# Two last-group steps of a graph layer with a mixture of experts moved forward, and its last block loaded, added and written in halves

## The chip, the cores and the metric

The kernel runs on one core of a Trainium2 chip. Its time is the device time of one launch in microseconds (us). Three timed runs of the kernel before gave 549.81, 551.37 and 551.41 us, median 551.37. A difference of under about 0.3% (1.65 us) can't be told from no change here.

## The reference

`x` has 4096 rows (nodes) of 256 values; `adj` is a 4096 by 4096 matrix of 0 and 1. Everything is float32.

```
x = x + gnn(layernorm(x), adj)
    # mask = adj > 0;  agg = mask @ h / max(row sums, 1)
    # relu(concat(h @ W_self + b_self, agg @ W_nb + b_nb) @ W_comb + b_comb)
x = x + ffn(layernorm(x))
    # logits = h @ Wg + bg;  top 2 of 8 experts, w = softmax of the two logits
    # y_e = gelu(h @ W1[e] + b1[e]) @ W2[e] + b2[e];  sum over the two of w * y_e
```

## The kernel before, in words

**Tiles and groups.** The 4096 rows are 32 tiles of 128 rows. Four tiles are a group (B = 4), and there are NG = 8 groups, numbered 0 to 7. "The last group" is group 7 (tiles 28 to 31), "the group in front" is group 6 (tiles 24 to 27).

**First stage: the graph layer and the routing.** Each engine has its own program, in which a function `main_step` is called once per step, and each call does one piece of work for several tiles at different ages (tile t-3, tile t-5 and so on). For each group, once its logits are there, four things happen in this order:

- *choose* (VectorE, `choose`, L911 to L926) finds the two best experts of each row. Its fourth instruction writes `dgap`, the gap of the two logits; its last ones write `both` and `base`, from which ranks are made.
- *powers* (GpSimd, `powers_of_e`, L555) computes e to the power of `dgap` into `egap`.
- *ranks* (TensorE, L1186 to L1189) are three small matmuls that count, for each row, how many rows before it go to the same expert.
- *slots* (VectorE, `slots`, L935 to L948) needs powers and ranks. It writes the two weights of each row and `slot`, the two places in the memory `dispatched` to which the row goes. It releases the semaphore `slots`.

Then GpSimd issues *dispatches* (L545): per tile two indirect DMAs of 128 rows of 260 values each, so eight per group. On GpSimd all of this stands in one list, made by a loop over s; before, the powers of group k come at step s = 4(k+3), that is s = 40 for group 7, behind the eight dispatches of group 6.

**Second stage: the experts.** The dispatched rows are worked off in ET = 39 expert tiles of 256 rows. Expert step t does, on TensorE: the transposes of tile t (L1211), the first product of tile t-1 (L1224), the second product of tile t-2 (L1239). VectorE copies transposed tiles (`exT`, L1028), makes low parts (L1042) and adds the bias (L1036); ScalarE does the gelu (L699), the high part (L704) and the weighting (L688). GpSimd scatters the weighted outputs to `pair_out` (L595, two indirect DMAs per tile). SyncE loads expert tiles (L466). The first EA = 9 tiles hold only rows of the first half of the groups, so they can run before the last groups are dispatched; from tile 9 on SyncE waits for all dispatches, for eight writes of pad rows (`write_pad`, L352 and L353, 260 KB each), and for the second part of a table that VectorE makes in its expert steps 1 to 4 (`table_late`, L990 to L1013). The pad writes in turn wait for `padrow`, the first instruction of `table_late(0)` (L990).

Where the two stages meet, two constants set the order: EARLY_PE = 2 expert steps stand on TensorE ahead of the last ranks, and EARLY_DVE = 1 on VectorE ahead of the last slots. TensorE's expert step 2 waits for the semaphore `slots` of the last group:

```
if known == EARLY_PE:
    pe.wait_ge(s_slot, NG)
```

**End.** For each group, SyncE waits for the scatters, loads the pairs of the group (`load_pairs`, L478, 1024 KB, from `pair_out` into one of four buffers), VectorE adds them to `x_sb` in two instructions (`combine`, L1066 and L1068), and SyncE writes the group out with four DMAs of 128 KB (`write_out`, L483). After the last group nothing else is left to do.

## Time and profile before

| | us |
|---|---|
| profiled execution, its time | 551.93 |
| profiled execution, its span | 550.1 |
| median of three timed runs | 551.37 |
| TensorE busy | 439.9 (80%) |
| VectorE busy | 391.1 (71%) |
| GpSimd busy | 288.2 (52%) |
| ScalarE busy | 272.6 (50%) |

The span is the time from the first to the last record of one profiled execution; 1.8 us of the execution's time lie around it. The page shows TensorE full from 50 us to 350 us (graph layer) and again from 400 us to 500 us (experts), with a thin stretch between, in which the routing of the last groups ends, and a thin end. The views of the next sections but one are timelines of one engine each: start, length, engine, line, operation, tiles, and in brackets how long the engine was idle before the row and what released it.

### The profile page before, as it was taken

The numbers are of one execution on the slowest core, as the hardware profiler recorded it, in microseconds if no ns is written. First come the engines' busy times: TensorE is split into PE (matmuls) and PEld (weight loads), VectorE is DVE, ScalarE is ACT, GpSimd is POOL, SyncE is SP. The second block draws the span as 40 slices with busy tenths as digits, with TensorE's granted clock in tenths as the row PEclk, the third lists the DMA queues.
The fourth block names the chain that finished last, engine by engine and source line by source line (L and its number), as shares of the span: only waits on it lengthen the run. The fifth ranks groups of instructions, "written<-read, shape, count | busy, mean of one in ns | idle before, by whom it ended". The sixth has DMA issues, their size and how long they took to land.

```text
span 550.1 us, 13137 instructions
## 1 busy us (share of the span) xinstructions
PE 439.9 (80%) x4321; PEld 382.9 (70%) x4321; DVE 391.1 (71%) x1197; ACT 272.6 (50%) x435; POOL 288.2 (52%) x305
## 2 busy tenths in 40 slices
PE   0015999999999999999999999635599999997730
PEld 0014889899898989898988898524378888786520
DVE  5717855686588888878857887574677777679871
ACT  3675452364255353654434444322367777776530
POOL 3993223234156575756564752646545556564570
PEclk9999999999999999999999999955989999999975
DMA  9975999999989999999996944512555555588565
GB/s 248 251 238 119 270 291 298 272 256 269 240 252 250 284 271 308 268 296 271 270 285 184 282 141 139 183 39 98 185 182 163 161 157 156 156 291 342 184 203 153
DMA packets 46785, 122.49 MB, mean 223 GB/s; under 512 B 8953, under 2 KB 18045, under 8 KB 45568
## 3 DMA queue, kind: packets, MB, share of 16 engines
q1 hardware_dynamic: 28896, 68.02, 47.4%
q0 software_dynamic: 16080, 50.49, 28.5%
q10 hardware_dynamic: 1744, 3.15, 2.1%
q8 instruction: 37, 0.61, 0.5%
q14 instruction: 28, 0.23, 0.1%
HBM read 96.52 MB, written 26.93 MB: 224 GB/s over the span
## 4 chain that ended last, share of the span: by engine, by line
PE 33%; DVE 15%; issue 15%; DMA 14%; POOL 13%; ACT 6%; SPq 1%; DVEq 1%; ACTq 1%; another core or an unknown queue 1%; POOLq 0%
PE bank L1224 8%; PE bank L1239 7%; PE bank L1115 5%; PE bank L1116 5%; DMA stage<-in_adj_dram,gidx 5%; POOL dispatched L545 4%; POOL stage L534 4%; DMA wst<-in_L_ffn_W_dram 4%; PE bank L1124 3%; PE bank L1211 2%; DMA stage<-in_adj_dram 2%; POOL z_lo L560 2%; DVE mask L769 2%; DMA x_sb<-in_x_dram 1%; DVE maskT L776 1%
## 5 line engine op out<-in xcount | busy, mean ns | idle before, releaser
L1115 PE MATMUL bank<-z_flat,maskT 128*128 128x257 f16 x1024 | 226.7, 273 | 0.0
L1116 PE MATMUL bank<-z_lo,maskT 128*128 128x256 f16 x1024 | 226.7, 273 | 0.0
L595 POOL DMA_INDIRECT pair_out<-rows,enum x78 | 80.9, 1038 | 64.8 <-DVE gate L1055 34.2
L534 POOL DMA_INDIRECT stage<-in_adj_dram,gidx x64 | 66.2, 1034 | 86.4 <-PE bank L1124 41.6
L1115 PEld LDWEIGHTS bank<-z_flat,maskT 128*128 128x128 fp8e4 x1024 | 100.2, 98 | 12.2
L1116 PEld LDWEIGHTS bank<-z_lo,maskT 128*128 128x128 fp8e4 x1024 | 100.2, 98 | 11.5
L545 POOL DMA_INDIRECT dispatched<-rows,slot x64 | 70.3, 1098 | 26.5 <-issue 19.2
L648 ACT ACTIVATE rows<-bank,rdeg 128x256 f16<-128x256 f32 x32 | 15.1, 473 | 134.3 <-DVE rdeg L829 110.7
L622 ACT ACTIVATE mask<-stage,m 128x2048 fp8e4<-128x2048 int32 x32 | 64.4, 2013 | 20.0 <-DMA stage<-in_adj_dram,gidx 17.9
L1224 PE MATMUL bank<-stage,w 128*128 128x256 f16 x468 | 61.3, 284 | 12.8 <-DVE stage L1028 11.0
L1239 PE MATMUL bank<-w,stage 128*128 x468 | 60.5, 278 | 9.9 <-DVE stage L1042 5.7
L577 POOL TENSOR_TENSOR rs<-ve,mhalf 128x1 f32<-128x1 f32 x32 | 34.9, 1091 | 61.2 <-DVE ve L853 60.1
L1239 PEld LDWEIGHTS bank<-w,stage 128*128 128x128 f16 x468 | 43.8, 99 | 24.6 <-issue 18.4
L699 ACT ACTIVATE stage<-bank,b1c,sc 128x256 f32<-128x256 f32 x78 | 40.2, 559 | 41.3 <-PE bank L1224 28.2
L1224 PEld LDWEIGHTS bank<-stage,w 128*128 x468 | 45.3, 101 | 20.6 <-issue 14.4
L1124 PE MATMUL bank<-wf,aT 128*128 128x256 f16 x384 | 47.2, 273 | 6.4 <-ACT aT L654 6.4
L776 DVE STREAM_TRANSPOSE maskT<-mask 128x1024 uint32<-128x1024 uint32 x32 | 39.9, 1245 | 13.7 <-ACT mask L622 10.5
L1124 PEld LDWEIGHTS bank<-wf,aT 128*128 128x128 f16 x384 | 37.2, 98 | 11.7 <-ACT aT L654 7.4
L769 DVE TENSOR_SCALAR mask<-stage 128x2048 fp8e4<-128x2048 int32 x32 | 39.2, 1226 | 7.4 <-DMA stage<-in_adj_dram 7.3
L688 ACT ACTIVATE rows<-rows,gate 128x256 f32<-128x256 f32 x78 | 35.1, 497 | 16.9 <-DVE rows L1036 13.2
L1028 DVE COPY stage<-bank 128x1024 f16<-128x1024 f16 x39 | 26.9, 690 | 23.1 <-PE bank L1224 16.7
L1042 DVE SCALAR_TENSOR_TENSOR stage<-stage,shs 128x512 f16<-128x512 f32 x39 | 29.2, 749 | 11.2 <-ACT stage L704 9.4
(175 smaller groups left out, 636.5 us busy)
## 6 DMA issues: line engine op xcount, KB each, us to landing
stage<-in_adj_dram SPq DMA_DIRECT2D x128, 256.0 KB
stage<-dispatched SPq DMA_DIRECT2D x39, 260.0 KB
wst<-in_L_ffn_W_dram SPq DMA_DIRECT2D x16, 256.0 KB
z_lo<-pair_out SPq DMA_DIRECT2D x4, 1024.0 KB
maskT<-pair_out SPq DMA_DIRECT2D x4, 1024.0 KB
out_dram<-x_sb SPq DMA_DIRECT2D x32, 128.0 KB
dispatched<-pad SPq DMA_DIRECT2D x15, 260.0 KB
x_sb<-in_x_dram SPq DMA_DIRECT2D x6, 256.0 KB, 9.1
```

What stands on the lines that cost most here:

```text
L534: gp.indirect_dma_start(out=stage[:, s, b - 2, :], out_offset=None, in_=adj_q[:, :], in_offset=bass.IndirectOffsetOnAxis(ap=gidx[:, 0:1], ...
L545: gp.indirect_dma_start(out=xs_dram[:, :], out_offset=bass.IndirectOffsetOnAxis(ap=slot[:, t, c:c + 1], axis=0), in_=rows_f[:, t, :], in_o ...
L595: gp.indirect_dma_start(out=yp_dram[:, :], out_offset=bass.IndirectOffsetOnAxis(ap=enum[:, a, s:s + 1], axis=0), in_=ysb[:, a, s, :], in_o ...
L622: sc.activation(mask[:, u % 2, 2:4, :], stage[:, s], ACT.Sigmoid, bias=m100[:, 0:1], scale=200.0, saturate=False).then_inc(s_mA, 1)
L699: sc.activation(ehid[:, u % 2, h, :], hps[2 * (u % 2) + h][:, 0:TT], ACT.Gelu, bias=b1c[:, bass.ds(ex, 1), h], scale=sc1[:, bass.ds(ex, 1) ...
L769: v.tensor_scalar(mask[:, u % 2, 0:2, :], stage[:, s], 0.0, None, ALU.is_gt, saturate=False).then_inc(s_mD, 1)
L776: v.transpose(maskT32[u % 4], mask32[u % 2]).then_inc(s_T, 1)
L1115: mm(acc[u % 2][:, 0:D + 1], a, z_hi[:, i, :], start=(i == 0), stop=False)
L1116: last = mm(acc[u % 2][:, 0:D], a, z_lo[:, i, :], start=False, stop=(i == NT - 1))
L1124: last = mm(out_, lhs(xp * KT + kt), w(wp, kt), start=(first and n == 0), stop=(final and n == 3 * KT - 1))
L1224: last = mm(hps[2 * r + h][:, 0:TT], w, exT[:, r, (xp * KT + kt) * TT:(xp * KT + kt + 1) * TT], start=(n == 0), stop=(n == 3 * KT - 1))
L1239: last = mm(fold[r][:, s * H:s * H + H], ehl[:, r, xp, kt, s * P:s * P + P], w, start=(n == 0), stop=(n == 3 * KT - 1))
```

## The change

The change has three parts.

1. On GpSimd the powers of group 7 stand at step s = 37, behind the powers of group 6 and ahead of the eight dispatches of group 6.
2. On TensorE the ranks of group 7 stand behind expert step 0 and ahead of expert step 1; before, they stood behind expert step 1. The wait for `slots` stays at expert step 2.
3. The pairs of group 7 are loaded in two DMAs of 512 KB with a semaphore each, added in two times two instructions of half the size, and written in two times four DMAs of 64 KB, the first half from SyncE, the second half from ScalarE.

```diff
-        LAST_RANKS, EARLY_PE, EARLY_DVE = NT + PR - B, 2, 1
+        LAST_RANKS, EARLY_PE, EARLY_DVE = NT + PR - B, 1, 1
...
+        def write_half(eng, h):
+            eng.wait_ge(s_o2, NG + h)
+            t = NT - B + h * B // 2
+            for g in range(G):
+                eng.dma_start(out_v[g, NG - 1, :, h * B // 2 * D:(h + 1) * B // 2 * D],
+                              x_sb[Q * g:Q * g + Q, t:t + B // 2, :].rearrange("p e d -> p (e d)")).then_inc(s_out, 16)
...
-                sp.dma_start(yin[k % Y].rearrange("p e k n -> p (e k n)"), yp_v[k]).then_inc(s_yl[k % Y], 16)
+                if k < NG - 1:
+                    sp.dma_start(yin[k % Y].rearrange("p e k n -> p (e k n)"), yp_v[k]).then_inc(s_yl[k % Y], 16)
+                else:
+                    for h in range(2):
+                        sp.dma_start(yin[k % Y][:, h * B // 2:(h + 1) * B // 2].rearrange("p e k n -> p (e k n)"),
+                                     yp_v[k, :, h * B * D:(h + 1) * B * D]).then_inc((s_yl[k % Y], s_yh)[h], 16)
...
-            for k in (NG - 2, NG - 1):
-                write_out(k)
-            sp.wait_ge(s_out, 16 * G * NG)
+            write_out(NG - 2)
+            write_half(sp, 0)
+            sp.wait_ge(s_out, 16 * G * (NG + 1))
...
+            LAST_POWERS = NT + X1
             sent = 0
             for s in range(GATE_STEPS + 1):
...
-                if s >= 12 and s % B == 0:
+                if s >= 12 and s % B == 0 and s // B - 3 < NG - 1:
                     powers_of_e(s // B - 3)
+                if s == LAST_POWERS:
+                    powers_of_e(NG - 1)
...
             for t in range(ET - GATED, ET):
                 gate_rows(t)
+            write_half(act, 1)
...
-            for k in range(len(COMBINE), NG):
+            for k in range(len(COMBINE), NG - 1):
                 combine(k)
+            for h in range(2):
+                dve.wait_ge(*((s_yl[Y - 1], 16 * (NG // Y)), (s_yh, 16))[h])
+                t, es = NT - B + h * B // 2, slice(h * B // 2, (h + 1) * B // 2)
+                xh_ = x_sb[:, t:t + B // 2, :]
+                v.tensor_tensor(xh_, xh_, yin[Y - 1][:, es, 0, :], ALU.add).then_inc(s_o1, 1)
+                dve.wait_ge(s_o1, NG + h)
+                v.tensor_tensor(xh_, xh_, yin[Y - 1][:, es, 1, :], ALU.add).then_inc(s_o2, 1)
...
-                if known == EARLY_PE:
+                if known == 2:
                     pe.wait_ge(s_slot, NG)
```

GpSimd, at the dispatches of groups 6 and 7. Before (the four dispatches ahead of the powers of group 7, the powers, the first dispatches of group 7):

```order
L545 DMA dispatched<-rows,slot 36608x260 [waits slots,hi2,lo2]
L545 DMA dispatched<-rows,slot 36608x260
L545 DMA dispatched<-rows,slot 36608x260 [waits slots,hi2,lo2]
L545 DMA dispatched<-rows,slot 36608x260
L555 TENSOR_TENSOR egap<-ebase,dgap 128x4 [waits logit_gaps]
L545 DMA dispatched<-rows,slot 36608x260 [waits slots,hi2,lo2]
L545 DMA dispatched<-rows,slot 36608x260
```

The same place now; the row with x2 holds the powers of groups 6 and 7, and the dispatches behind it are those of group 6, with those of group 7 right behind them (`rs` is the inverse deviation of the second layernorm):

```order
L592 TENSOR_TENSOR rs<-ve,mhalf 128x1 [waits variance2] x2
L568 TENSOR_TENSOR egap<-ebase,dgap 128x4 [waits logit_gaps] x2
L558 DMA dispatched<-rows,slot 36608x260 [waits slots,hi2,lo2]
L558 DMA dispatched<-rows,slot 36608x260
L558 DMA dispatched<-rows,slot 36608x260 [waits slots,hi2,lo2]
L558 DMA dispatched<-rows,slot 36608x260
```

The powers of group 7 moved ahead of eight dispatches, and the sixteen dispatches of the two groups now follow one another.

TensorE, where the two stages meet. Before: transposes of expert tile 0, transposes of tile 1, the first product of tile 0 (L1224, of whose rows the first two and the last one are shown), the last ranks (L1186 to L1189), then expert step 2 with its wait for `slots`:

```order
L1211 MATMUL bank<-ident,stage 128x128 [waits expert_rows_loaded0,expert_lo,tables]
L1211 MATMUL bank<-ident,stage 128x128 x7
L1211 MATMUL bank<-ident,stage 128x128 [waits expert_rows_loaded1]
L1211 MATMUL bank<-ident,stage 128x128 x7
L1224 ISA [waits e_transposed_copied]
L1224 MATMUL bank<-stage,w 128x256
L1224 MATMUL bank<-stage,w 128x256
L1186 MATMUL bank<-both,upper 128x32 [waits expert_scales,one_hots]
L1187 MATMUL bank<-base,ones 128x32
L1189 MATMUL bank<-base,ones 128x8
L385 TENSOR_LOAD tab [waits slots]
```

The same place now, with the product cut in the same way:

```order
L1236 MATMUL bank<-ident,stage 128x128 [waits expert_rows_loaded0,expert_lo,tables]
L1236 MATMUL bank<-ident,stage 128x128 x7
L1211 MATMUL bank<-both,upper 128x32 [waits expert_scales,one_hots]
L1212 MATMUL bank<-base,ones 128x32
L1214 MATMUL bank<-base,ones 128x8
L1236 MATMUL bank<-ident,stage 128x128 [waits expert_rows_loaded1]
L1236 MATMUL bank<-ident,stage 128x128 x7
L1249 ISA [waits e_transposed_copied]
L1249 MATMUL bank<-stage,w 128x256
L1249 MATMUL bank<-stage,w 128x256
L385 TENSOR_LOAD tab [waits slots]
```

The ranks moved ahead of the transposes of tile 1 and of the first product; the wait for `slots` stayed behind that product.

## Rows read from the trace of the kernel before

**Rows 1.** Windows: busy us (x) of PE PEld DVE ACT POOL, PEclk, DMA share, GB/s.
```profile
360.00:380.00 20.00, 6.40 (x60) 5.13 (x60) 9.67 (x55) 5.31 (x9) 10.38 (x11) 0.50 0.15 55
...
410.00:420.00 10.00, 9.59 (x99) 8.12 (x97) 7.30 (x18) 7.77 (x16) 5.60 (x7) 1.00 0.61 167
```

**Rows 2.** Timeline of GpSimd, 366 to 391 us, in part.
```profile
366.72 1.03 POOL L545 DMA_INDIRECT dispatched<-rows,slot  x1 [2.82 <-DVE slot L948]
...
376.69 1.04 POOL L555 TENSOR_TENSOR egap<-ebase,dgap 128x4 f32<-128x4 f32 x1
380.14 1.02 POOL L545 DMA_INDIRECT dispatched<-rows,slot  x1 [2.41 <-DVE slot L948]
...
388.04 1.35 POOL L545 DMA_INDIRECT dispatched<-rows,slot  x1 [0.30 <-issue]
389.69 0.97 POOL L545 DMA_INDIRECT dispatched<-rows,slot  x1 [0.30 <-issue]
```

**Rows 3.** Timeline of VectorE, 367 to 392 us, in part.
```profile
367.03 0.17 DVE L913 TENSOR_TENSOR dgap<-top 128x4 f32<-128x4 f32 x1
...
369.70 0.68 DVE L1028 COPY stage<-bank 128x1024 f16<-128x1024 f16 x1
377.77 0.17 DVE L935 TENSOR_SCALAR wden<-egap 128x4 f32<-128x4 f32 x1 [7.39 <-POOL egap L555]
...
379.15 0.17 DVE L948 CAST slot<-slotf 128x8 int32<-128x8 f32 x1
380.69 0.74 DVE L1042 SCALAR_TENSOR_TENSOR stage<-stage,shs 128x512 f16<-128x512 f32 x1
...
381.68 0.16 DVE L990 TENSOR_TENSOR padrow<-cntt,region 128x8 int32<-128x8 f32 x1
...
387.14 1.41 DVE L1003 TENSOR_TENSOR z_lo<-tio,z_lo 128x1200 f32<-128x1200 f32 x1
...
391.95 0.69 DVE L1028 COPY stage<-bank 128x1024 f16<-128x1024 f16 x1 [1.98 <-remote]
```

**Rows 4.** Timeline of TensorE, 366 to 392 us, in part.
```profile
366.09 1.89 PE L1211 MATMUL bank<-ident,stage 128*128 128x128 f16 x16
370.52 2.74 PE L1224 MATMUL bank<-stage,w 128*128 128x256 f16 x12 [2.54 <-DVE stage L1028]
373.05 0.23 PE L1186 MATMUL bank<-both,upper 128*128 128x32 f16 x1
...
380.03 1.03 PE L1211 MATMUL bank<-ident,stage 128*128 128x128 f16 x8 [6.71 <-DVE slot L948]
...
387.71 0.71 PE L1239 MATMUL bank<-w,stage 128*128 x5
...
391.79 0.60 PE L1239 MATMUL bank<-w,stage 128*128 x4 [0.45 <-issue]
```

**Rows 5.** Timeline of ScalarE, 374 to 392 us, in part.
```profile
374.12 0.72 ACT L704 ACTIVATE stage<-stage,shs 128x512 f16<-128x512 f32 x1
...
392.21 1.02 ACT L699 ACTIVATE stage<-bank,b1c,sc 128x256 f32<-128x256 f32 x2 [7.18 <-remote]
```

**Rows 6.** SyncE's instructions of line 352, 384 to 392 us.
```profile
L352 SPq SEQ_ASSERT  x3: 14/649/699, 383.6 to 391.0; - x3
```

**Rows 7.** Waits of SyncE's queue, whole span, one row.
```profile
SPq L463 <- DVE tab L1013: 3.8, 1, 3.8
```

**Rows 8.** Timeline of all engines, 535 to 546 us.
```profile
535.45 0.99 POOL L595 DMA_INDIRECT pair_out<-rows,enum  x1 [0.30 <-issue]
537.75 0.34 SPq L478 DMA_DIRECT2D maskT<-pair_out  x1
538.14 9.81 SPq L483 DMA_DIRECT2D out_dram<-x_sb  x8
543.73 1.22 DVE L1066 TENSOR_TENSOR x_sb<-x_sb,maskT 128x1024 f32<-128x1024 f32 x1 [8.31 <-DMA maskT<-pair_out]
544.98 1.23 DVE L1068 TENSOR_TENSOR x_sb<-x_sb,maskT 128x1024 f32<-128x1024 f32 x1
```

More of the change, by code:

```diff
@@ L291, in gnn_moe_kernel @@
         s_ysc = [sem(f"outputs_scattered{i}") for i in range(RY)]
-        s_padr = sem("pad_places")
+        s_padr, s_yh = sem("pad_places"), sem("last_half_of_pairs_loaded")
         s_g2, s_gt = sem("gate_steps"), sem("outputs_weighted")
```

## The prediction

> **What bounds the kernel now.** I read the page's slices and the windows first, then the chain of waits, then each engine's timeline where the chain leaves TensorE. Through most of the span TensorE is the bound, in the expert stage too: in 410 to 420 us it is busy 9.59 of 10 us at a granted clock of 1.00 [rows 1]. Two stretches are not its own. From 360 to 380 us it is busy 6.40 of 20 us at a clock of 0.50 [rows 1], and there the chain runs over GpSimd: the slots of group 7 start only at 377.77, after VectorE has idled 7.39 us for `egap` [rows 3], which GpSimd makes at 376.69, behind the eight dispatches of group 6 that began at 366.72 [rows 2]. TensorE idles 6.71 us for these slots before the transposes of tile 2 at 380.03 [rows 4]. The second stretch is the end: last scatter 535.45 to 536.44, pairs of group 7 asked for at 537.75, added from 543.73 to 546.21 [rows 8], span over at 550.1, 3.9 us later.
>
> A third feature decides how much of the first stretch comes back. From about 387 to 392 us engines stand still though what they wait for is there. TensorE has done five of twelve matmuls of a second product at 388.42 and does the last four at 391.79 [rows 4]; ScalarE is idle 7.18 us until 392.21, though its input, the first half of the product that ended ahead of TensorE's row of 387.71, was ready at about 387.1 [rows 4, 5]; a check on SyncE's sequencer that can take 14 ns takes 649 and 699 ns [rows 6]; a copy on VectorE waits 1.98 us until 391.95 [rows 3]. The first pad writes and the last dispatches (389.69 plus 0.97 us, [rows 2]) are under way together there. It ends about a microsecond after the last dispatch.
>
> **Part 1, powers ahead of the dispatches.** `dgap` of group 7 is ready at 367.03 + 0.17 = 367.20 [rows 3]. The powers now start there and take 1.04 [rows 2], to 368.3. The dispatches of group 6 start 0.3 later, at 368.6 instead of 366.72: 1.9 us late. Nobody waits for them but the tiles from 9 on, which wait for all dispatches. Eight of them at 0.97 + 0.30 us give 378.8 for the first dispatch of group 7, instead of 380.14: 1.3 us early, since the 2.41 us of waiting and the 1.04 us of powers go and 1.9 us come. The last dispatch ended at 390.66; it now ends at 389.3, or at about 390.1 if two more of them are as slow as the one of 1.35 us.
>
> That slow dispatch at 388.04 ran beside a VectorE instruction with two inputs, 387.14 to 388.55 [rows 2, 3]. The Trainium skill ("SBUF — State Buffer", "SBUF: two separate sides") says that such a VectorE instruction and a GpSimd operation that reads the same memory lock each other out entirely. By that rule this dispatch would end 0.97 after 388.55, at 389.52; it ended at 389.39, so the trace nearly agrees. By that rule moving sixteen dispatches beside VectorE's table work gives back up to 0.8 of the 1.3 us; without it the 1.3 us stay. It doesn't change the slots.
>
> **Part 2, ranks ahead of the first product.** Before, the ranks stood at 373.05, behind the product of 370.52 [rows 4]; with the powers at 368.3 they would have been the next wait. Now they start when VectorE's choose is done, about 369.8, and take some 0.3. TensorE's transposes of tile 1 (half of 16 in 1.89 us, or 1.03 for eight at 380.03, [rows 4]) now stand behind them, so the first product starts at 371.1 instead of 370.52: 0.6 late. VectorE's copy of tile 0 (369.70 to 370.38) keeps its place, then the slots take 379.32 - 377.77 = 1.55 [rows 3]: ready at 372.0 instead of 379.32, 7.3 early.
>
> What is late next is the chain of tile 0: its high part ended at 374.12 + 0.72 = 374.84 on ScalarE [rows 5], now at 375.4, and the low part on VectorE, which stood at 380.69 [rows 3], follows at 375.5. That is 5.2 early. TensorE's transposes of tile 2 follow the product at 373.9, 6.1 early, and wait no more. `padrow` (381.68, [rows 3]) and with it the pad writes are 5.2 early too. So 5.2 us reach the standstill.
>
> **The standstill.** Its place in the work is fixed by the pad writes, 5.2 early; its end, if it hangs on pads and dispatches together, by the last dispatch, which is only 1.3 early. I can't price this from one row, so both ends: 5.2 us if it travels with the work and keeps its length, 1.3 if nothing moves until the dispatches are out. I take 3.0, nearest to ScalarE's row, since the chain goes through ScalarE there: its instruction went 5.1 us after its input was ready, not never. Input ready 5.2 early (381.9) plus 5.1 gives 387.0; its gelus and high part take 1.9 free, and three more such 0.65 us delays bring them to 390.9, where before they ended at 394.07. That is 3.2; TensorE's row alone (three matmuls in 3.4 us) would give some 1.7. Hence 3.0.
>
> Behind it nothing else is known to hold the work: tile 9's load waited last for the table, 3.8 us [rows 7], and the table is VectorE work of expert steps 1 to 4, so it moves with the rest; in the full stretch [rows 1] a shift stays a shift.
>
> **Part 3, halves.** Before, the adding took 2.48 us behind the whole load [rows 8]. An instruction of 512 elements costs between half of 1.22, 0.61, and 0.74, the low part's [rows 8, 3]. Two for the first half run while the second half still comes in; two for the second, some 1.4 us, stay behind the end of the load: 1.1 us saved. The last four writes carry half the bytes and start from ScalarE, idle by then; their issue (546.21 to 547.95, [rows 8]) keeps its 1.7 us, the last landing saves perhaps 0.2. Sum 1.3. Lower bound: both halves land together and all four additions stay, about -0.1. Upper: 2.0, if the shorter second load also lands sooner. The extra DMA issue costs 0.34 us ahead of group 6's writes [rows 8], which aren't last.
>
> Issue to first addition was 5.98 us for 1024 KB, beside 512 KB of writes [rows 8]. The Trainium skill ("DMA: Bandwidth & Descriptors", "Anatomy of one DMA — SWDGE (gpsimd) path") gives a DMA a fixed 2.0 us and the rest by bytes at 436 GB/s. By it 512 KB would be in after 3.2 us and 1024 KB after 4.4, so halves would lead by 1.2 us, a little short of the 1.4 that the first two additions need; the saving would be 0.9. The trace's longer time speaks for more lead. It is stated for GpSimd's DMAs, and no row here shows a half by itself.
>
> **Sum.** 3.0 + 1.3 = 4.3 us off the profiled execution's 551.93: 547.6. That execution stands 0.56 above the median of the runs, so for the median 551.37 - 4.3 = 547.1.
>
> **Rivals.**
> 1. *The standstill travels with the work.* It needs a cause in the work or the pads alone. For it: it begins behind the first pad writes, and dispatches alone don't stop TensorE's product at 370.52 [rows 4]. Against: it ends with the dispatches. 5.2 + 1.3 = 6.5, to 544.9.
> 2. *The standstill is a wall.* Everyone resumes behind the last dispatch: 1.3 + 1.3 = 2.6, to 548.8; 549.6 with the slow dispatches.
> 3. *The front gain is lost at tile 9.* SyncE has pads, dispatches and table to wait for; were pads beside twice as many dispatches as slow as now, the full stretch would start when it does now. Against: 3.8 us of slack towards the table [rows 7]. Only the end is left: 550.1.
> 4. *Slower.* Pads now meet nearly all eight dispatches instead of the last four. If each meeting costs both sides, six dispatches at 1.8 us instead of 1.27 end at 392.5, and if TensorE did nothing in between it would resume 2 us later than now with about 2 us less done: 4 lost, 1.3 won, 554.1. It decides only when the last dispatch ends well after 390.66; the one row of 1.35 us [rows 2] speaks for much less.
> 5. *The change doesn't do what it says:* `egap` is one buffer for all groups, and powers of group 7 directly behind those of group 6 would have to wait for the slots of group 6. VectorE runs those ahead of `dgap` of group 7 (GpSimd's row of 366.72 was released by them, [rows 2]), so no.
>
> **Chances.** Forecast 0.45 (its own range 545.9 to 548.5), rival 1 0.27, rival 2 0.14, rival 3 0.09, rival 4 0.05. The range takes in rival 1 with its bounds and rival 2 with its slow dispatches: 544.1 to 549.9. A change is told from none beyond 0.3%, 1.65 us, so "faster" means under 549.7: 0.45 + 0.27 + most of rival 2 = 0.83. The same: 0.12, rival 3 and a little of rival 2. Slower 0.05.
>
> **What the profile of the changed kernel would show.** GpSimd: `egap` of group 7 near 367.3, sixteen dispatches in a row from 368.6, the last ending between 389 and 390.5. VectorE: slots of group 7 done near 372. TensorE: ranks near 370, the idle of 6.71 us gone, clock high before 380. The low part of tile 0 near 375.5 and `padrow` near 376.5. Then the test: matmuls of the second product of tile 1, and ScalarE's gelus of tile 2, stretched out and resuming near 387 (rival 1), near 390.5 (rival 2) or in between. Tile 9 loaded about 3 us before 403.5. At the end first addition of half a group about 1.4 us ahead of the load's end, and less than 3.9 us from last addition to the end of the span. I'm wrong if the slots are early and the low part of tile 0 isn't, if the last dispatch ends after 391, or if both halves land together.

## The result, and the profile after

The change made the kernel slower. After: 554.64 us, median of 8 runs (552.7 to 555.7). Before, on the same chip: 550.54 us, median of 8 runs (548.08 to 554.16). The recorded ratio is 1.0095, 95% interval 1.0071 to 1.0119; the two medians alone give 1.0074. Every ratio in this document leaves out the executions that lie over 1.5% above the fastest of the same kernel in their session; in e10 these are five of twelve, elsewhere at most three. The profiled execution of the changed kernel took 555.3 us, its span is 553.4 us, the mean granted clock 0.943.

All rows of this section are of the changed kernel. GpSimd first (start, length, engine, line, operation, tiles; in brackets the idle time before and what released it):

```profile
364.98 1.01 POOL L568 TENSOR_TENSOR egap<-ebase,dgap 128x4 f32<-128x4 f32 x1 [3.38 <-DVE dgap L931]
366.17 1.03 POOL L558 DMA_INDIRECT dispatched<-rows,slot  x1 [0.17 <-issue]
...
377.74 1.59 POOL L558 DMA_INDIRECT dispatched<-rows,slot  x1 [0.31 <-issue]
...
386.01 0.97 POOL L558 DMA_INDIRECT dispatched<-rows,slot  x1 [0.31 <-issue]
```

The powers stand directly behind `dgap`, and the sixteen dispatches run in one row, about 1.27 us from start to start. In [rows 2] they were eight, then the powers and 2.4 us of waiting, then eight. VectorE:

```profile
364.74 0.17 DVE L931 TENSOR_TENSOR dgap<-top 128x4 f32<-128x4 f32 x1
369.23 0.17 DVE L966 CAST slot<-slotf 128x8 int32<-128x8 f32 x1
376.44 0.75 DVE L1060 SCALAR_TENSOR_TENSOR stage<-stage,shs 128x512 f16<-128x512 f32 x1 [5.59 <-issue]
377.45 0.16 DVE L1008 TENSOR_TENSOR padrow<-cntt,region 128x8 int32<-128x8 f32 x1
377.66 0.82 DVE L1011 TENSOR_TENSOR z_lo<-cntt,q 128x640 f32<-128x640 f32 x1
391.53 0.75 DVE L1060 SCALAR_TENSOR_TENSOR stage<-stage,shs 128x512 f16<-128x512 f32 x1 [8.88 <-ACT stage L721]
...
405.14 0.19 DVE L1031 SCALAR_TENSOR_TENSOR tab<-tio,tjmp 128x30 int32<-128x30 f32 x1
```

In this execution `dgap` was ready 2.3 us earlier than in [rows 3]. The change moves nothing ahead of it, and over all profiles here its start lies anywhere from 361.5 to 367.0 us, so I count from `dgap`. The slots end 4.7 us behind the start of `dgap`, where they ended 12.3 behind it in [rows 3]: 7.6 early. `padrow` stands 12.7 behind it instead of 14.65: only 1.9 early. The last piece of the table, L1031, stands 40.4 behind it; before it stood 35.5 behind it, 4.9 us less (402.51 in the trace of before, where `dgap` stood at 367.03). So the gain is lost, and more, between `padrow` and the table. TensorE and ScalarE there:

```profile
369.27 2.77 PE L1249 MATMUL bank<-stage,w 128*128 128x256 f16 x12
...
377.34 2.52 PE L1264 MATMUL bank<-w,stage 128*128 x12 [2.42 <-DVE stage L1060]
...
381.24 0.22 PE L1236 MATMUL bank<-ident,stage 128*128 128x128 f16 x1 [0.74 <-issue]
...
387.81 0.37 PE L1249 MATMUL bank<-stage,w 128*128 128x256 f16 x1 [1.74 <-issue]
389.35 2.08 PE L1249 MATMUL bank<-stage,w 128*128 128x256 f16 x9 [1.17 <-issue]
```

```profile
374.87 0.57 ACT L716 ACTIVATE stage<-bank,b1c,sc 128x256 f32<-128x256 f32 x1 [3.37 <-PE bank L1249]
375.58 0.72 ACT L721 ACTIVATE stage<-stage,shs 128x512 f16<-128x512 f32 x1
389.52 1.02 ACT L716 ACTIVATE stage<-bank,b1c,sc 128x256 f32<-128x256 f32 x2 [13.22 <-remote]
```

From 381.24 to 387.81 TensorE issues single matmuls 1.4 to 2.1 us from start to start, idle 0.7 to 1.7 us before each, with nothing to wait for that the profile shows ("issue"). ScalarE does nothing for 13.22 us, where [rows 5] show 7.18; "remote" says that the profile found the releaser on none of this core's engines. The standstill of the kernel before is still there; it begins earlier and is longer. Its first sign is earlier still: ScalarE takes the second half of the first product at 374.87, 2.8 us after that product is over (369.27 plus 2.77 is 372.04). Two windows (columns as in [rows 1]):

```profile
360.00:380.00 20.00, 11.42 (x88) 8.80 (x86) 11.43 (x61) 4.92 (x8) 13.32 (x14) 0.59 0.20 65
380.00:390.00 10.00, 2.60 (x14) 1.30 (x13) 1.23 (x4) 0.48 (x2) 5.46 (x6) 0.67 0.46 165
```

From 360 to 380 us TensorE is now busy 11.42 us instead of 6.40 [rows 1]: the change works there. In the next 10 us it is busy 2.60. SyncE:

```profile
384.23 12.57 SPq L353 DMA_DIRECT2D dispatched<-pad  x8
406.18 3.91 SPq L474 DMA_DIRECT2D stage<-dispatched  x4
```

SyncE's check of line 352, one before each pad write (count, then shortest, median and longest in ns, first and last start in us):

```profile
L352 SPq SEQ_ASSERT  x8: 18/18/710, 381.2 to 396.1; - x8
```

The first pad write is issued at 384.23, behind the first stretched rows of TensorE, and the check that takes 18 ns in the median takes up to 710. Tile 9 is loaded at 406.18; 41.4 us behind `dgap`. The tail, in which group 7 is loaded at L490, added at L1099 and L1101 and written at L404:

```profile
540.24 0.99 POOL L612 DMA_INDIRECT pair_out<-rows,enum  x1 [0.31 <-issue]
542.52 0.82 SPq L490 DMA_DIRECT2D maskT<-pair_out  x2
546.99 0.69 DVE L1099 TENSOR_TENSOR x_sb<-x_sb,maskT 128x512 f32<-128x512 f32 x1 [6.66 <-DMA maskT<-pair_out]
547.72 0.69 DVE L1101 TENSOR_TENSOR x_sb<-x_sb,maskT 128x512 f32<-128x512 f32 x1
548.44 0.69 DVE L1099 TENSOR_TENSOR x_sb<-x_sb,maskT 128x512 f32<-128x512 f32 x1
549.17 0.69 DVE L1101 TENSOR_TENSOR x_sb<-x_sb,maskT 128x512 f32<-128x512 f32 x1
```

From the start of the last scatter to the end of the span it is 13.2 us, before 14.65 [rows 8]: 1.5 us won.

The spans add up so: `dgap` 2.3 early, `dgap` to table 4.9 longer, table to the end 148.3 instead of 147.6, so 0.7 longer in spite of the 1.5 won in the tail (the 2.2 lost on the way there are not taken apart here). That is 3.3 us, the difference of the spans (553.4 and 550.1).

### The profile page after: what moved, and what is told of

Same layout as the page of the kernel before. It is cut to its first block, busy times and chain, and to the rows that moved or that the text cites. A ratio compares the mean times of both kernels' runs of the same rounds, so it can differ in the third digit from the quotient of the medians.

```text
span 553.4 us, 13144 instructions
## 1 busy us (share of the span) xinstructions
PE 447.6 (81%) x4321; PEld 387.4 (70%) x4321; DVE 390.5 (71%) x1199; ACT 273.1 (49%) x435; POOL 286.0 (52%) x305
## 3 DMA queue, kind: packets, MB, share of 16 engines
q10 hardware_dynamic: 1936, 3.41, 2.2%
## 4 chain that ended last, share of the span: by engine, by line
DVE 30%; issue 17%; PE 16%; DMA 14%; ACT 11%; POOL 5%; another core or an unknown queue 2%; SPq 1%; DVEq 1%; ACTq 1%; POOLq 0%
DMA wst<-in_L_ffn_W_dram 7%; PE bank L1249 7%; PE bank L1264 6%; DMA stage<-in_adj_dram 4%; DVE mask L787 4%; DVE maskT L794 3%; ACT aT L671 2%; PE bank L1236 2%; DVE stage L1060 2%; POOL z_lo L573 2%; ACT mask L639 2%; ACT xT L677 2%; DVE st L866 2%; DVE xh L840 1%
## 5 line engine op out<-in xcount | busy, mean ns | idle before, releaser
L1249 PE MATMUL bank<-stage,w 128*128 128x256 f16 x468 | 64.2, 289 | 13.2 <-issue 7.1
L1264 PE MATMUL bank<-w,stage 128*128 x468 | 63.4, 288 | 10.8 <-DVE stage L1060 9.1
L639 ACT ACTIVATE mask<-stage,m 128x2048 fp8e4<-128x2048 int32 x32 | 64.5, 2015 | 13.2 <-DMA stage<-in_adj_dram,gidx 10.3
L592 POOL TENSOR_TENSOR rs<-ve,mhalf 128x1 f32<-128x1 f32 x32 | 33.1, 1034 | 60.8 <-DVE ve L871 59.1
L1264 PEld LDWEIGHTS bank<-w,stage 128*128 128x128 f16 x468 | 45.1, 102 | 26.6 <-issue 18.8
L1060 DVE SCALAR_TENSOR_TENSOR stage<-stage,shs 128x512 f16<-128x512 f32 x39 | 29.2, 750 | 26.9 <-ACT stage L721 18.4
```

The lines of the kernel that those rows point to most:

```text
L639: sc.activation(mask[:, u % 2, 2:4, :], stage[:, s], ACT.Sigmoid, bias=m100[:, 0:1], scale=200.0, saturate=False).then_inc(s_mA, 1)
L1249: last = mm(hps[2 * r + h][:, 0:TT], w, exT[:, r, (xp * KT + kt) * TT:(xp * KT + kt + 1) * TT], start=(n == 0), stop=(n == 3 * KT - 1))
L1264: last = mm(fold[r][:, s * H:s * H + H], ehl[:, r, xp, kt, s * P:s * P + P], w, start=(n == 0), stop=(n == 3 * KT - 1))
```

## The experiments

**How to read them.** Each comparison is made against runs of the kernel before on the same chip in the same session, and the sessions differ: the kernel before took about 550 us in the result's session, 550.67, 548.70 and 548.57 us in sessions 2, 3 and 4, and 534.62, 535.80 and 534.78 us in sessions 1, 5 and 6. I call the former long sessions and the latter short ones. What sets them apart these runs don't tell. The record gives sessions 3 and 6 the same chip number, 5, and the one was long, the other short; if the number stands for the same chip both times, the chip alone doesn't set them apart. As a measure inside a profile I use the interval from the start of `dgap` of group 7 to the start of the last piece of the table (L1031 in the changed kernel): everything the front of the change touches lies in it, and what came before it doesn't. Each interval is that of one profiled execution, and how much it scatters was not measured. "Standstill" is the longest idle time of ScalarE from 370 to 396 us that the profile puts down to "remote" or "issue"; it misses idle that the profile puts down to an engine that was already done, as at 374.87 above.

| session | kernel | ratio (95%) | dgap to table, us | standstill, us |
|---|---|---|---|---|
| result | before | 1 | 35.5 | 7.2 |
| result | the change | 1.0095 (1.0071 to 1.0119) | 40.4 | 13.2 |
| 1, short | e1 part 3 alone | 0.9963 (0.993 to 0.9996) | 32.8 | none |
| 1, short | e2 parts 1 and 2 | 0.9931 (0.9895 to 0.9968) | 28.4 | none |
| 1, short | e3 part 1 alone | 0.9918 (0.9884 to 0.9952) | 28.0 | none |
| 1, short | e4 part 2 alone | 1.0008 (0.9975 to 1.0042) | 32.8 | none |
| 2, long | e5 the change | 1.0057 (1.0018 to 1.0096) | 40.2 | 13.7 |
| 3, long | e6 one break of 3.4 us | 0.996 (0.9929 to 0.9992) | 33.9 | 6.2 |
| 3, long | e7 pads held | 1.0046 (1.0012 to 1.008) | 39.7 | 11.4 |
| 3, long | e8 paced | 1.0067 (1.0035 to 1.0098) | 28.0 | 2.6 |
| 3, long | e9 part 1 alone | 1.0076 (1.0041 to 1.011) | 39.9 | 8.3, twice |
| 4, long | e10 one short break | 0.9933 (0.989 to 0.9976) | 32.6 | 6.1 |
| 4, long | e11 two breaks | 0.9937 (0.9901 to 0.9972) | 31.1 | 2.7 |
| 4, long | e12 before, row of 8 broken | 0.9944 (0.9914 to 0.9974) | 32.9 | 2.8 |
| 5, short | e13 the change | 0.9894 (0.9852 to 0.9936) | 28.5 | none |
| 5, short | e14 one short break | 0.9883 (0.9842 to 0.9924) | 28.9 | none |
| 5, short | e15 three short breaks | 0.9876 (0.9841 to 0.991) | 28.6 | none |
| 5, short | e16 e12 again | 1.0007 (0.9976 to 1.0037) | 33.2 | none |
| 6, short | e17 the change | 0.9887 (0.9856 to 0.9918) | 28.4 | none |
| 6, short | e18 three short breaks | 0.9905 (0.9868 to 0.9942) | 28.7 | none |

### Session 1: the parts apart

e1 keeps only part 3:

```diff
-        LAST_RANKS, EARLY_PE, EARLY_DVE = NT + PR - B, 1, 1
+        LAST_RANKS, EARLY_PE, EARLY_DVE = NT + PR - B, 2, 1
-            LAST_POWERS = NT + X1
+            LAST_POWERS = B * (NG + 2)
```

> Only part 3 of the change (last pairs loaded, added, written in halves) on the kernel before. Theory A (the loss is a standstill of the sequencers that comes from sixteen dispatches of GpSimd in one row, so from part 1; part 3 gains as forecast): about 1.3 to 1.5 us faster than before, profile: last scatter to end of span 13.2 us instead of 14.65. Rival B (part 3 costs, for instance by its extra DMAs or by moving every engine's program text): slower than before by 1 us or more.

e2 keeps parts 1 and 2; the pairs of group 7 are loaded, added and written whole:

```diff
-                if k < NG - 1:
+                if k < NG:
...
-            write_half(act, 1)
...
-            for k in range(len(COMBINE), NG - 1):
+            for k in range(len(COMBINE), NG):
...
```

> Parts 1 and 2 (powers early, ranks early) without part 3. Theory A: the standstill is there as in the changed kernel (ScalarE idle some 13 us until about 2 us behind the last dispatch), time about 1.4 us above the changed kernel, that is some 5 to 6 us above before. Rival B (part 3 costs): faster than the changed kernel.

e3 is e2 without part 2, e4 is e2 without part 1; each has the edits of e2 and this one:

```diff
(e3)
-        LAST_RANKS, EARLY_PE, EARLY_DVE = NT + PR - B, 1, 1
+        LAST_RANKS, EARLY_PE, EARLY_DVE = NT + PR - B, 2, 1
(e4)
-            LAST_POWERS = NT + X1
+            LAST_POWERS = B * (NG + 2)
```

> Only part 1: powers of group 7 ahead of the dispatches of group 6, ranks where they were. Theory A: sixteen dispatches in one row, standstill of 8 to 13 us, 3 to 6 us slower than before. Rival C (the loss comes from part 2: ranks and transposes of tile 1 ahead of the first product): at most 1 us from before, or faster by up to 4 us since the slots come early.

> Only part 2: ranks of group 7 ahead of expert step 1, powers where they were, so the slots still wait for the powers behind eight dispatches. Theory A: two rows of eight dispatches with a gap of some 3 us, as before; time as before within 1 us. Rival C (part 2 costs): 3 us or more slower than before.

The session was a short one, and no kernel showed a standstill. There the front gained 3.6 us (e2, 531.02 against 534.62), the halves 2.0 (e1), part 1 alone as much as both (e3, 3.4), part 2 alone nothing (e4). The interval to the table says the same: 32.8 without part 1, 28.4 and 28.0 with it. So the losses expected of e2 and e3 didn't come, and the parts are not slow in themselves; what made the change slower in the first measurement was missing here.

### Session 2: the change again

e5 is the changed kernel, unedited.

> The changed kernel once more, unchanged, to see whether its place against the kernel before is one number. In the first comparison it stood at 554.64 against 550.54; in the second, where before stood at 534.62, parts 1 and 2 alone gained 3.6 us and part 3 alone 2 us. Theory D (the loss belongs to a state of the chip in which engines stand still beside GpSimd's dispatches; where that state is absent the forecast's gain appears): with before near 534, the change stands 5 to 6 us below it and its profile shows no idle of ScalarE put down to remote around 370 to 390 us; with before near 550, it stands 3 to 5 us above it and shows that idle. Rival E (the three parts together cost what none costs alone): slower than before in either case.

553.16 against 550.67 us: slower again, with the same picture, ScalarE idle 13.71 us until 389.52.

### Session 3: breaks, pads, pace

e6 puts three small powers, 3.41 us of GpSimd's time, between the dispatches of groups 6 and 7 (`fill`, here and below, is a tile of its own that nothing reads):

```diff
                     if sent < B * ((s - SLOT) // B + 1):
+                        if sent == NT - B:
+                            for i in range(3):
+                                gp.tensor_tensor(fill[:, 4 * i:4 * i + 4], ebase[:, :, 0], mhalf[:, :], ALU.pow)
                         dispatch(sent)
```

> The changed kernel with three extra powers of GpSimd (about 3.1 us together, into an unused tile) between the eight dispatches of group 6 and those of group 7, so that the row of sixteen has the break that it had before. Where before stands near 550 us: theory F (engines crawl once a row of dispatches runs without a break for some ten us, until about 2.5 us behind its last one): the standstill shrinks from some 13 us of ScalarE idle to 5 to 7, time 3 to 6 us below the changed kernel. Rival H (whatever expert work runs beside dispatches crawls, break or not): the standstill lasts until 2.5 us behind the last dispatch, which is now 3 us later, and the time is 2 to 3 us above the changed kernel. Where before stands near 535 us, there is no standstill and the time is that of the changed kernel, or up to 1.5 us above.

e7 holds the pad writes until all dispatches have landed:

```diff
                     sp.wait_ge(s_padr, 1)
+                    sp.wait_ge(s_sc[1], 16 * NT)
...
                     sp.wait_ge(s_tab, 4)
-                    sp.wait_ge(s_sc[1], 16 * NT)
```

> The changed kernel with the eight pad writes held until all dispatches have landed. Near 550 us: rival G (the standstill of my forecast: pad writes and dispatches under way together): no standstill between 372 and 389 us, some 5 us or more below the changed kernel. Theories F and H: the standstill stays as it is, since it begins before the first pad write; time within 2 us of the changed kernel.

e8 puts one power behind each of the sixteen dispatches:

```diff
+                    if t >= NT - 2 * B:
+                        i = 4 * (2 * (t - (NT - 2 * B)) + c)
+                        gp.tensor_tensor(fill[:, i:i + 4], ebase[:, 0:4, 0], mhalf[:, 0:4], ALU.pow)
```

> The changed kernel with one extra power of GpSimd (1.03 us, into an unused tile) behind each of the sixteen dispatch DMAs of groups 6 and 7, so that one comes every 2.3 us instead of every 1.27 and the last ends near 403. Near 550 us: theory F in the form that the rate matters: no standstill, slots early and expert steps at their pace from 372 us on; 6 to 10 us below the changed kernel, tile 9's load just in time. Rival H: crawl until 405 us, 10 us or more above the changed kernel. Near 535 us: 0 to 4 us above the changed kernel, by tile 9's later load.

e9 is e3 again, in a long session.

> Only part 1 (powers early), as in e3, to have it beside a kernel before near 550 us if this chip gives that. Theories F and H: sixteen dispatches in one row beside expert steps, 4 to 7 us slower than before; near 535 us: 3 us faster, as in e3.

e7, ScalarE, then SyncE:

```profile
385.29 0.57 ACT L716 ACTIVATE stage<-bank,b1c,sc 128x256 f32<-128x256 f32 x1 [11.38 <-remote]
```

```profile
388.14 7.15 SPq L353 DMA_DIRECT2D dispatched<-pad  x6
```

The pad writes come only at 388.14, behind the standstill, and it is there all the same, and the kernel is slower than before. They are not its cause. Here ScalarE is back at 385.29, before the last dispatch ends (385.87); in the change it came back 2.5 us after it.

e6, GpSimd at the break, then ScalarE:

```profile
373.45 0.96 POOL L559 DMA_INDIRECT dispatched<-rows,slot  x1 [0.30 <-issue]
374.43 3.41 POOL L607 TENSOR_TENSOR fill<-ebase,mhalf 128x4 f32<-128x4 f32 x3
378.03 1.03 POOL L559 DMA_INDIRECT dispatched<-rows,slot  x1 [0.19 <-issue]
```

```profile
376.14 1.02 ACT L720 ACTIVATE stage<-bank,b1c,sc 128x256 f32<-128x256 f32 x2 [2.33 <-remote]
...
393.09 1.02 ACT L720 ACTIVATE stage<-bank,b1c,sc 128x256 f32<-128x256 f32 x2 [6.23 <-remote]
```

ScalarE comes back in the break and stands still again behind the second row of eight, about as long as in [rows 5]. More work on GpSimd, and the kernel is 1.4 us faster than before by the medians (547.32 against 548.70) instead of slower: the interval is 33.9 us beside 39.7 and 39.9 for the unbroken rows of e7 and e9 in the same session. e9's ScalarE shows where those stand:

```profile
379.09 0.56 ACT L716 ACTIVATE stage<-bank,b1c,sc 128x256 f32<-128x256 f32 x1 [8.26 <-remote]
387.68 0.56 ACT L716 ACTIVATE stage<-bank,b1c,sc 128x256 f32<-128x256 f32 x1 [8.03 <-remote]
```

e8 had an interval of 28.0 us, as short as in a short session, and lost it behind tile 9. GpSimd, TensorE and ScalarE:

```profile
401.06 1.03 POOL L559 DMA_INDIRECT dispatched<-rows,slot  x1 [0.21 <-issue]
402.11 1.04 POOL L564 TENSOR_TENSOR fill<-ebase,mhalf 128x4 f32<-128x4 f32 x1
403.35 1.03 POOL L616 DMA_INDIRECT pair_out<-rows,enum  x1 [0.20 <-DVE gate L1077]
...
417.45 0.97 POOL L616 DMA_INDIRECT pair_out<-rows,enum  x1 [0.30 <-issue]
```

```profile
407.32 1.03 PE L1240 MATMUL bank<-ident,stage 128*128 128x128 f16 x8 [5.73 <-DMA stage<-dispatched]
```

```profile
412.02 0.56 ACT L720 ACTIVATE stage<-bank,b1c,sc 128x256 f32<-128x256 f32 x1 [8.81 <-PE bank L1253]
419.05 0.56 ACT L720 ACTIVATE stage<-bank,b1c,sc 128x256 f32<-128x256 f32 x1 [6.46 <-remote]
```

The last dispatch is issued at 401.06, tile 9 is loaded behind it, and TensorE waits 5.73 us. The scatters that had piled up behind the dispatches then run in one unbroken row from 403.35 on, and the standstill is back beside them. No dispatch is in that row of twelve: in this one execution a row of scatters did what the rows of dispatches do. The expected 6 to 10 us of gain didn't come; the kernel was 0.67% slower than before.

### Session 4: how much of a break

e10 has one power between the groups, e11 two powers ahead of the seventh and two ahead of the thirteenth dispatch, and e12 is the kernel before with two powers in the middle of group 7's eight dispatches. The diff is that of e10, with the values of the other two as comments:

```diff
                     if sent < B * ((s - SLOT) // B + 1):
+                        if sent in (NT - B,):                    # e11: (NT - 5, NT - 2), e12: (NT - 2,)
+                            for i in range(1):                   # e11 and e12: 2
+                                gp.tensor_tensor(fill[:, 4 * (i + 3 * (NT - sent)):4 * (i + 3 * (NT - sent)) + 4], ebase[:, :, 0], mhalf[:, :], ALU.pow)
                         dispatch(sent)
```

> The whole change, with one extra small power on GpSimd (about 1.14 us) between the last dispatch of group 6 and the first of group 7, where the earlier run had three (3.4 us). Theory (an unbroken row of sixteen dispatches starts the standstill): if any break will do, the standstill of 13 us on ScalarE is cut as with three powers (waits of 2 to 6 us), the last dispatch ends 2.2 us earlier than there, and the time is 1 us or more below before. If the break has to be long enough for the queue to drain, one power is too short: ScalarE stands still 10 us or more until about 2.5 us after the last dispatch, and the ratio is 1.005 or above. Rival (the place of group 7's dispatches beside expert tile 0 counts, not the break): nearly as the change itself, 1.005 to 1.01.

> The whole change, with two breaks of two extra powers (2.3 us each) in the row of sixteen dispatches: before the seventh and before the thirteenth, so rows of six, six and four. Theory (the length of the unbroken row decides): no row is longer than 7 us, so no standstill over 3 us on ScalarE between 370 and 395, the expert tiles keep their pace, and the time is 3 to 4.5 us below before (ratio 0.992 to 0.995), more than the 1.4 us that one break gave, unless the 1.2 us later last dispatch costs it at tile 9. Rival (the sum of dispatches in flight decides, not breaks): as with one break, 0.996. Second rival (any dispatch beside expert tiles costs the same): 1.005.

> The kernel before, with one break of two extra powers (2.3 us) in the middle of group 7's eight dispatches, so rows of four and four there. Theory: its standstill of 5.2 us at ScalarE behind that row goes or shrinks to 2 us or less, while the last dispatch ends 2.3 us later; if tile 9 isn't held by it, the time is 1 to 4 us below before (0.993 to 0.998). Rival (the standstill of before comes from the pad writes and dispatches together, as first thought): it stays near 5 us, and moves 2.3 us later, ratio 1.000 to 1.004.

One short break cut the longest such idle of ScalarE to 6.1 us, where the change had 13.2 in the first measurement, two breaks cut it to 2.7 and the interval to 31.1 us. In e12 the standstill of the kernel before is gone too: 32.9 us, the interval of its front in the short sessions (32.8), no "remote" wait, and 0.9944 with nothing changed but 2 us more work on GpSimd. All three ratios lie within each other's intervals, so their order isn't told. e10's gain itself is not firm: its twelve executions reach from 541.05 to 553.04 us, and the median of all of them is 547.40 against 548.57, 0.2% below before; the ratio of 0.9933 counts the seven lowest. In e11 all twelve count (median 544.05), in e12 too (545.02).

In e11 something of the standstill is left. ScalarE takes the second half of the first product 2.7 us after that product is over (it starts at 375.64, the product ends at 372.91), and behind the last four dispatches four scatters follow without a break, so that a row of eight runs from 387.23 to 398.85; ScalarE then idles 3.87 us on "remote" until 406.77, outside the stretch of the table above. e10, GpSimd at its break:

```profile
374.45 1.35 POOL L559 DMA_INDIRECT dispatched<-rows,slot  x1 [0.31 <-issue]
375.82 1.35 POOL L607 TENSOR_TENSOR fill<-ebase,mhalf 128x4 f32<-128x4 f32 x1
377.37 1.02 POOL L559 DMA_INDIRECT dispatched<-rows,slot  x1 [0.20 <-issue]
```

### Sessions 5 and 6: the change beside the breaks

e13 and e17 are the changed kernel; e14 is e10 again, e16 is e12 again; e15 and e18 have one power after the fourth, eighth and twelfth dispatch (`if sent in (NT - 6, NT - B, NT - 2)` in the diff above).

> The change as it is, beside the three kernels with breaks, so that they share a chip and the runs of before. Theory (its unbroken row of sixteen dispatches makes the standstill): ratio 1.005 to 1.010, ScalarE without an instruction for 10 us or more between 376 and 392. Rival (the breaks of the last runs gained because that chip stands still less, not by the breaks): the change is below before here too, ratio 0.993 to 0.998, level with the kernels with breaks.

> The change with the one short break (one extra power of about 1.1 us) between the last dispatch of group 6 and the first of group 7. Theory: 0.993 to 0.997 where the change itself is 1.005 or more, so 1 to 1.5% between the two on the same chip. Rival: level with the change within 0.3%.

> The change with three short breaks (one extra power each) in the sixteen dispatches: after the fourth, the eighth and the twelfth. Rows of four. Theory: the least standstill of all, no instruction pause of ScalarE over 3 us between 378 and 395 that is not a wait for TensorE at its pace, and 0.989 to 0.993. If the breaks' 3.4 us are lost at tile 9 again (its load waits for the last dispatch), level with one break, 0.994 to 0.997.

> The kernel before with two extra powers in the middle of group 7's eight dispatches, for the comparison with the change plus breaks on one chip. It gave 0.9944 on its own chip. If the earlier ranks and the halves are worth what the chip without standstills showed (about 3.6 and 2 us), the change with three breaks is 2 us or more below this one. If this one is level or below, the place of the breaks is all there is to win, and the earlier powers and ranks bring nothing here. Expected 0.993 to 0.996.

> The change as it is, beside the kernel with three short breaks. If this chip is of the kind with standstills (before at 548 us or more): ratio 1.005 to 1.010, ScalarE without an instruction for 10 us or more. If it is of the other kind (before near 535 us): 0.987 to 0.993, as on the last chip.

> The change with breaks of one extra power after the fourth, eighth and twelfth dispatch. On a chip with standstills the theory wants 0.989 to 0.996, at least 1% below the change beside it, with no standstill over 6 us on ScalarE before 395. The rival (the gain of the kernels with breaks came from their chip) wants both level within 0.3%. On a chip without standstills both are level, near 0.989, and it decides nothing.

Both sessions were short ones. e13, GpSimd, ScalarE and VectorE:

```profile
363.37 1.03 POOL L558 DMA_INDIRECT dispatched<-rows,slot  x1 [0.17 <-issue]
...
384.56 1.35 POOL L558 DMA_INDIRECT dispatched<-rows,slot  x1 [0.30 <-issue]
```

```profile
369.41 0.56 ACT L716 ACTIVATE stage<-bank,b1c,sc 128x256 f32<-128x256 f32 x1 [0.70 <-PE bank L1249]
...
378.69 0.56 ACT L716 ACTIVATE stage<-bank,b1c,sc 128x256 f32<-128x256 f32 x1 [5.89 <-PE bank L1249]
...
383.73 1.02 ACT L716 ACTIVATE stage<-bank,b1c,sc 128x256 f32<-128x256 f32 x2
```

```profile
372.05 0.16 DVE L1008 TENSOR_TENSOR padrow<-cntt,region 128x8 int32<-128x8 f32 x1
...
390.40 0.19 DVE L1031 SCALAR_TENSOR_TENSOR tab<-tio,tjmp 128x30 int32<-128x30 f32 x1
```

SyncE's check, which took up to 710 ns in the first measurement:

```profile
L352 SPq SEQ_ASSERT  x8: 18/18/18, 373.8 to 384.0; - x8
```

The same kernel and the same unbroken row of sixteen, and no standstill: ScalarE only waits for TensorE. The change gains 1.1% (529.31 against 535.80 us) and again in session 6 (0.9887). Breaks add nothing (e13, e14 and e15 within 0.2%; e17 and e18 too), and e16 gains nothing. So the breaks help only where there is a standstill; the unbroken row alone doesn't make one. Later in e13 GpSimd even issues 34 indirect DMAs in one unbroken row, from 400.61 to 451.7 us, and ScalarE has no idle over 2.5 us on "remote" or "issue" there. What stays missing is a long session with the change itself beside a kernel with breaks: both sessions meant for it were short ones. The nearest is session 3, where e7 and e9, with the unbroken row, lie 0.9% and 1.2% above e6.

Of these kernels the change with a break is the one to keep, and which break is open. One short break took 0.9883 (0.9842 to 0.9924) of before in a short session, level with the change; in a long one its ratio was 0.9933 (0.989 to 0.9976), but 0.998 by the medians of all executions. Two breaks are the firmest gain in a long session (0.9937, 0.9901 to 0.9972) and were not run in a short one.

## Why the prediction was wrong

**Part 1** was right on GpSimd: powers behind `dgap`, sixteen dispatches in a row. The last ended 22.2 us behind the start of `dgap` (386.98), where I had said 22 to 23.5 (389 to 390.5, `dgap` at 367.03). The slow dispatch of 1.59 us at 377.74 stood beside VectorE's two-input row of 377.66 to 378.48. The rule of the Trainium skill ("SBUF — State Buffer", "SBUF: two separate sides") would have it end 0.97 behind that, at 379.45; it ended at 379.33, so it agrees to 0.1 us, as the row in [rows 2] did. It doesn't hold for every row of that kind: beside VectorE's L1060 from 376.44 to 377.19, which reads two operands from the same memory too, the dispatch of 376.46 took its plain 0.97. What I didn't ask is what the row of sixteen does to the other engines. I priced the break between the groups as waiting that goes away, and it was what kept the standstill short.

**Part 2** was right on its own terms: slots 7.6 us early, forecast 7.3. But it was credited with a gain that part 1 brings alone (e3 28.0, e2 28.4 us to the table; e4 none). The clock forecast to be high before 380 was so in part: from 370 to 380 us the granted clock was 0.67 in the mean, 0.50 before, and from 380 to 390, in the standstill, 0.67 where it had been 0.84.

**The low part of tile 0 and `padrow`** were forecast 5.2 early. With the standstill `padrow` came 1.9 early. TensorE's first product ran at its pace (2.77 us), but ScalarE took its second half 2.8 us after its end, and in e13 0.2 us after it (369.41, the product over at 369.25). Without the standstill `padrow` was 10.1 us behind `dgap` in e13 and 14.6 in e1, which has the front of before: 4.5 early. The working held where nothing stood still.

**"The standstill" is the step that failed**, in place and in price. I wrote that "its place in the work is fixed by the pad writes" and took a gain of 3.0, between 1.3 and 5.2. Measured from `dgap` to the table it was a loss of 4.9. The pad writes don't cause it (e7). In the sessions that have it, it hangs on the unbroken row of indirect DMAs: it came earlier and stayed longer because the row grew from eight to sixteen (the change, e5, e7, e9: 39.7 to 40.4 us), and it shrank where the row was broken (e6, e10, e11: 31.1 to 33.9; e12 against before: 32.9 against 35.5). The price of that is 40.4 - 28.4 = 12 us of interval for the change and 35.5 - 32.8 = 2.7 for before, with the short sessions as the floor; the 4.4 us that the front wins on that floor are lost to a price that is 9.3 higher, which leaves the 4.9. The bounds were worked out as a question of when one given standstill ends; that it could begin earlier was in no case. The row that spoke for it was among those I read: TensorE's second product broke off at 388.42 [rows 4], some eight us into group 7's row of dispatches [rows 2]. I read the pads into it because they were under way there too. And I wrote that it begins behind the first pad writes, which the trace of before doesn't bear out. SyncE there:

```profile
385.92 12.91 SPq L353 DMA_DIRECT2D dispatched<-pad  x8
```

The first pad write was issued at 385.92, and the first of SyncE's slow checks, 0.65 us, had started at 383.6 [rows 6].

**Part 3** was right: forecast 1.3, 1.5 in the tail of the first comparison, 2.0 in e1's time (interval 0.2 to 3.7). The additions take 0.69 each, and the halves didn't land together: the second was in at 548.42, 1.4 us after the first addition began. From the load's issue to the first addition it was 4.47 us (542.52 to 546.99) instead of the 5.98 of [rows 8]. By the rule of the Trainium skill ("DMA: Bandwidth & Descriptors", "Anatomy of one DMA — SWDGE (gpsimd) path") the data would be in, an estimate, after 3.2 us instead of 4.4; both measured times are longer than its figures, but the lead of 1.5 us lies near its 1.2.

**The rivals.** Rival 4 gave 554.1 us, close to the 554.64 measured, but by luck: it wanted pads that slow the dispatches down; the last dispatch ended no later than forecast, and e7 rules the pads out. What is right in it is its second half, that TensorE does nothing in between. Rival 3 is what befell e8, not the change: in the changed kernel tile 9 waited for the table, not for dispatches. Rival 1 gives the number of the short sessions best, though not their mechanism, since no standstill travels there: front and halves together gained 6.5 and 5.2 us (e13, e17), and it had forecast 6.5.

**What stays open.** Why some sessions show the standstill and others don't, and which resource it is. TensorE, ScalarE and SyncE slow down together, SyncE in instructions that move no data (710 ns for a check of 18), so it is not one engine's data path; GpSimd itself keeps its 1.27 us. The Trainium skill ("Runtime: NRT & Kernel Launch", "Instruction fetch mechanics") says that each sequencer fetches its instructions over a DMA queue of its own. Fetches that queue behind the descriptors of a long row of indirect DMAs would look like this, and I have not tested it. The page of the changed kernel lists two DMA queues of the kind "instruction", q8 with 37 packets and 0.61 MB and q14 with 28 and 0.23. Neither has a packet from 371.5 to 398.9 us. That would fit a fetch that waits, but TensorE was back at its pace from 389.35, over 9 us before the next packet, so none of these packets ended the standstill, which speaks against it. From 376 to 392 us the kernel before has none either, while e13, without a standstill, has three. Whose queues they are, and whether every engine's are among them, the profile doesn't say.

## What to carry to other kernels

Before you close a gap in an engine's list, ask what the gap gives the others: here 3.5 us without an indirect DMA on GpSimd were worth more than the 7.6 us by which the slots came early. Where several engines idle on "issue" or "remote" at once beside a long back-to-back row of GpSimd DMAs, try one small instruction in the middle of the row before anything else; here one power, 1.35 us of GpSimd, took the longest such idle from 13.2 to 6.1 us, the changed kernel with one or two breaks stood 0.2 to 0.7% below before where the change alone had stood 0.6 to 0.95% above (in other sessions), and where there was no standstill one or three breaks cost nothing. Measure such a change in more than one session: the same two kernels stood at +0.95% and at -1.1%.

## What the runs showed of the hardware

- The kernel before took 548.6 to 550.7 us in four sessions and 534.6 to 535.8 in three, with nothing in between; the same changed kernel in e5 and e13 differs by 24.8 us of span, of which 3.0 lie ahead of `dgap`, 11.7 between `dgap` and the table, and 10.1 behind.
- Beside an unbroken row of sixteen indirect DMAs, 1.27 us apart, in a long session the other engines issue one instruction per 1.4 to 2.1 us (TensorE, 381.24 to 387.81) or none for 13.2 us (ScalarE), until 2.5 us after the last of the row (386.98 to 389.52); in e7 ScalarE was back 0.6 us before the row's end. SyncE's check takes up to 710 ns there, 18 ns in e13. Beside rows of four or six dispatches no such idle between 370 and 396 us was over 2.8 us (e11, e12). A row of twelve scatters had it too, 6.5 us of ScalarE (e8). In a short session neither sixteen dispatches nor a row of 34 indirect DMAs brings it (e13).
- A GpSimd dispatch beside a two-input VectorE instruction of 0.82 us (L1011) took 1.59 us instead of 0.97; beside another of 0.75 us (L1060) it took 0.97.
